# Zeroing the masked triangle on GpSimd after the exponential, in place of a mask matmul before it

## What is computed

```python
def _L1_attn_ref(x, ...):
    ...
    scores = jnp.einsum('bhqd,bhkd->bhqk', q_full, k_full) * scale
    causal = jnp.tril(jnp.ones((T, T), dtype=bool))
    scores = jnp.where(causal[None, None], scores, -jnp.inf)
    probs = jax.nn.softmax(scores, axis=-1)
    y = jnp.einsum('bhqk,bhkd->bhqd', probs, v)
...
x = x + _L1_attn_ref(xn, ...) + _L1_ffn_ref(xn, ...)
```

## Time and profile before

| | us |
|---|---|
| median of 3 runs | 770.57 |
| lowest, highest | 769.31, 770.59 |
| profiled execution | 769.39 |
| its span | 767.6 |
| busy: PE, PEld, DVE, ACT, POOL | 676.4, 541.6, 513.2, 395.2, 355.9 |

### The profile page before, as it was taken

One profiled execution on the slowest core, in us unless ns is written; L12 is line 12 of the kernel. 1 busy time (PEld: TensorE's weight loads), 2 busy tenths in 40 slices (PEclk: granted clock), 3 DMA queues, 4 the chain that ended last, 5 costly groups with the idle time before them and its releaser, 6 DMA issues.

```text
span 767.6 us, 13256 instructions
## 1 busy us (share of the span) xinstructions
PE 676.4 (88%) x4656; PEld 541.6 (71%) x4656; DVE 513.2 (67%) x964; ACT 395.2 (51%) x695; POOL 355.9 (46%) x299
## 2 busy tenths in 40 slices
PE   5898789896976799989989999989989998999996
PEld 4676666886865677767677777667767777777774
DVE  6875746874776656686584867485749577467745
ACT  3644414453552654482765374575446286448263
POOL 1426088386585424153445445164516353315353
PEclk9999899998998999999999999999999999999999
DMA  8336816676976285420005202003303000202100
GB/s 318 115 112 218 266 75 213 211 229 221 340 247 202 77 298 130 158 63 22 2 2 145 49 18 66 2 1 100 94 2 76 9 1 29 73 12 50 34 2 28
DMA packets 66804, 82.76 MB, mean 108 GB/s; under 512 B 7090, under 2 KB 50354, under 8 KB 66738
## 3 DMA queue, kind: packets, MB, share of 16 engines
q1 hardware_dynamic: 63156, 73.39, 30.2%
q0 software_dynamic: 3072, 8.39, 3.3%
q10 hardware_dynamic: 512, 0.13, 0.1%
HBM read 40.34 MB, written 28.84 MB: 90 GB/s over the span
## 4 chain that ended last, share of the span: by engine, by line
PE 43%; ACT 11%; DVE 10%; issue 7%; DMA 2%; POOL 1%; ACTq 1%; SPq 0%; POOLq 0%; DVEq 0%
PE acc L643 4%; PE acc L645 3%; PE acc L644 3%; PE pv L643 3%; PE pm L643 3%; PE ring L965 2%; PE pm L645 2%; PE pm L644 2%; PE pv L645 2%; PE pv L644 2%; DVE hf L2115 2%; PE ring L995 2%; DMA ws<-qs 2%; PE ring L967 2%; ACT act L1448 1%
## 5 line engine op out<-in xcount | busy, mean ns | idle before, releaser
L1558 POOL TENSOR_TENSOR hl<-hf,hh 128x512 fp32r<-128x512 f32 (+1 forms) x76 | 99.2, 1307 | 227.3 <-ACT hh L1247 227.2
L1247 ACT ACTIVATE hh<-hf 128x512 fp32r<-128x512 f32 (+1 forms) x76 | 47.7, 629 | 81.7 <-DVE hf L2115 66.5
L643 PE MATMUL acc<-hh,wh 128*128 128x512 f32 (+1 forms) x168 | 71.1, 423 | 7.6 <-POOL hl L1558 7.6
L2179 DVE TENSOR_REDUCE mx<-ring 128x2 f32<-128x512 f32 (+1 forms) x96 | 61.5, 682 | 9.2 <-PE ring L967 9.2
L645 PE MATMUL acc<-hl,wh 128*128 128x512 f32 (+1 forms) x168 | 66.7, 397 | 0.0
L644 PE MATMUL acc<-hh,wl 128*128 128x512 f32 (+1 forms) x168 | 66.7, 397 | 0.0
L2115 DVE TENSOR_TENSOR hf<-hf,pv 128x512 f32<-128x512 f32 x64 | 43.6, 681 | 34.0 <-PE pv L645 32.6
L1699 POOL TENSOR_TENSOR pl<-act,ph 128x512 f16<-128x512 f32 x32 | 41.6, 1301 | 39.7 <-ACT ph L1453 36.8
L1430 ACT ACTIVATE hf<-pm 128x512 f32<-128x512 f32 x56 | 33.3, 595 | 51.5 <-PE pm L645 51.3
L643 PE MATMUL pv<-xh,wh 128*128 128x512 f32 x128 | 53.7, 419 | 1.8 <-DVE hf L2115 1.5
L645 PE MATMUL pv<-xl,wh 128*128 128x512 f32 x128 | 50.5, 395 | 0.0
(11 more groups left out here) (288 smaller groups left out, 2124.3 us busy)
## 6 DMA issues: line engine op xcount, KB each, us to landing
w4s<-w4hl SPq DMA_DIRECT2D x16, 512.0 KB, 4.5
ws<-qs SPq DMA_DIRECT2D x12, 512.0 KB, 6.0
qT<-qp SPq DMA_DIRECT2D x96, 64.0 KB
kT<-kp SPq DMA_DIRECT2D x96, 64.0 KB
xs<-yg SPq DMA_DIRECT2D x2, 2944.0 KB, 12.4
late<-xs SPq DMA_DIRECT2D x22, 256.0 KB, 3.4
ys<-act SPq DMA_DIRECT2D x22, 256.0 KB, 4.1
stage<-w SPq DMA_DIRECT2D x8, 608.0 KB, 4.6
```

The lines of the kernel that those rows point to most:

```text
L643: pe.matmul(o, w_hi, x_hi, start=first, stop=False, skip_group_check=True)
L1247: a.activation(h_parts(n)[0][0:rows, :], hf[0:rows, n % 2, :], ACT.Copy).then_inc(s_hh, 1)
L1558: return pool.tensor_tensor(dst, src, hi.bitcast(F32), ALU.subtract)
L2179: v.tensor_reduce(mx[:, i, h0:h0 + nh], ring[j % 2][:, :].rearrange("p (n k) -> p n k", n=nh), AX.X, ALU.max).then_inc(s_mx, 1)
```

## The change

The mask matmul and its constant go. Behind each exponential POOL issues one `affine_select`, in place in the fp32 buffer: over the diagonal squares of the fill (two of 128 x 128, or four), it keeps an element where query index - key index >= 0 and writes 0 elsewhere. Both halves of the split now wait for this select (semaphore `triangles_cleared`). On ACT the high half of fill f-1 comes behind the exponential of fill f; on POOL the low half of fill f-2 comes behind the select of fill f. `probs_hi` on DVE waits for the select too. The loads of the small constants are one fewer.

```diff
@@ PE, probs @@
-                        pe.matmul(o, kT[0:SLOT + 2, h, kt * P:(kt + 1) * P], qT[0:SLOT + 2, h, kt * P:SEQ], start=True,
-                                  stop=False, skip_group_check=True)
-                        mm = pe.matmul(o[:, 0:P], ident[:, :], maskk[:, :], start=False, stop=True,
-                                       skip_group_check=True)
+                        mm = pe.matmul(o, kT[0:SLOT + 2, h, kt * P:(kt + 1) * P], qT[0:SLOT + 2, h, kt * P:SEQ],
+                                       start=True, stop=True, skip_group_check=True)
@@ ACT @@
                 a.activation(exps(n), ring[f % 2][:, :], ACT.Exp, scale=SCALE).then_inc(s_e, 1)
-                if n % 3 != 1:
-                    a.wait_ge(s_e, n + 1)
-                    if n >= NP:
-                        a.wait_ge(s_y, (n - NP) // 3 + 1)
-                    a.activation(ph[:, n % NP, :], exps(n), ACT.Copy).then_inc(s_pha, 1)
+
+            def probs_hi(nb, f):
+                n = 12 * nb + f
+                a.wait_ge(s_sel, n + 1)
+                if n >= NP:
+                    a.wait_ge(s_y, (n - NP) // 3 + 1)
+                a.activation(ph[:, n % NP, :], exps(n), ACT.Copy).then_inc(s_pha, 1)
...
                     for f in fills:
                         exponentials(nb, f)
+                        if f and (f - 1) % 3 != 1:
+                            probs_hi(nb, f - 1)
+                        if f == 11:
+                            probs_hi(nb, 11)
@@ POOL @@
+                def clear_triangles(nb, f):
+                    n, heads = 12 * nb + f, 4 if f % 3 == 2 else 2
+                    pool.wait_ge(s_e, n + 1)
+                    square = exps(n).rearrange("p (h q) -> p h q", h=heads)[:, :, 0:P]
+                    pool.affine_select(square, square, [[0, heads], [1, P]], ALU.is_ge, 0.0, base=0,
+                                       channel_multiplier=-1).then_inc(s_sel, 1)
+
+                def probs_part(nb, *fills):
+                    for f in fills:
+                        clear_triangles(nb, f)
+                        if f >= 2 and (f - 2) % 3 != 2:
+                            probs_lo(nb, f - 2)
...
-                probs_lo(b0, 0, 1)
+                probs_part(b0, 0, 1, 2, 3)
                 split_h(n0 + 7, P)
-                probs_lo(b0, 3, 4, 6, 7, 9, 10)
+                probs_part(b0, *range(4, 12))
+                probs_lo(b0, 10)
@@ DVE, probs_hi @@
-                v.wait_ge(s_e, n + 1)
+                v.wait_ge(s_sel, n + 1)
```

More of the change, by code:

```diff
@@ L198, in transformer_blocks @@
         maskq = sb("maskq", [P, P], BF16, c1)
-        maskk = sb("maskk", [P, P], BF16, c1)
         ys = sb("ys", [P, 8, DH + 1], F32, c1)
@@ L290, in transformer_blocks @@
         s_md, s_vsp = sem("max_placed"), sem("values_split")
-        s_sT, s_e, s_y, s_yst, s_yn = map(
-            sem, ("score_bank_turned", "exponentials", "y_bank", "y_steps", "y_normed"))
+        s_sT, s_e, s_sel, s_y, s_yst, s_yn = map(
+            sem, ("score_bank_turned", "exponentials", "triangles_cleared", "y_bank", "y_steps", "y_normed"))
         s_ytr, s_yh, s_yl, s_ao = map(sem, ("y_turned", "y_hi", "y_split", "y_used"))
@@ L518, in small_in @@
                           (gb[:, :], cols), (bout[:, :], bo), (spreadf[:, :], spread_c),
-                          (ident[:, :], identb_c.bitcast(BF16)), (maskq[:, :], mask_c[0].bitcast(BF16)),
-                          (maskk[:, :], mask_c[1].bitcast(BF16)))[i]
+                          (ident[:, :], identb_c.bitcast(BF16)), (maskq[:, :], mask_c.bitcast(BF16)))[i]
                 sp.dma_start(t, src).then_inc(s_const if i else s_bc, 16)
@@ L579, in _ @@
                     x_in(5)
-                if 6 <= q < 14:
+                if 6 <= q < 13:
                     small_in(q - 6)
@@ L952, in scores @@
                         if nb == 0:
-                            pe.wait_ge(s_const, 16 * 9)
+                            pe.wait_ge(s_const, 16 * 8)
                             pe.wait_ge(s_prep, SETUP0 + SETUP1)
@@ L1391, in affine_latents @@
                 if nb == 0:
-                    a.wait_ge(s_const, 16 * 9)
+                    a.wait_ge(s_const, 16 * 8)
                 a.wait_ge(s_ctr, nb + 1)
@@ L1723, in _ @@
                     split_h(n0 + t, P)
-                probs_lo(b1, 0, 1)
+                probs_part(b1, 0, 1, 2, 3)
                 split_h(n0 + 13, P)
-                probs_lo(b1, 3, 4, 6, 7, 9, 10)
+                probs_part(b1, *range(4, 12))
+                probs_lo(b1, 10)
                 split_h(n0 + 14, P)
@@ L2136, in turn_bias @@
             def turn_bias():
-                v.wait_ge(s_const, 16 * 9)
+                v.wait_ge(s_const, 16 * 8)
                 v.tensor_tensor(bqc[:, :, :], gb[:, C_BQ:C_BQ + 4].rearrange("p (i m) -> p i m", i=2),
@@ L2419, in _layouts @@
     bf16 = lambda c: (c.view(np.uint32) >> 16).astype(np.uint16)
-    masks = np.zeros((2, P, P), f)
-    masks[0][np.triu_indices(P, 1)] = MASKED
-    masks[1][np.tril_indices(P, -1)] = MASKED
+    mask = np.zeros((P, P), f)
+    mask[np.triu_indices(P, 1)] = MASKED
     route_c = np.zeros((P, R_COLS), f)
@@ L2433, in _layouts @@
         "ones_c": np.full((P, P), 1.0 / D, f), "ident_c": np.eye(P, dtype=f),
-        "identb_c": bf16(np.eye(P, dtype=f)), "mask_c": bf16(masks), "route_c": route_c,
+        "identb_c": bf16(np.eye(P, dtype=f)), "mask_c": bf16(mask), "route_c": route_c,
         "ones_rows": bf16(np.ones((2, H * SEQ), f)).reshape(2, H, SEQ),
```

## The result

| | median us | runs | range | profiled run / span |
|---|---|---|---|---|
| before | 770.58 | 4 | 769.31 to 771.45 | 769.39 / 767.6 |
| after | 810.19 | 4 | 808.75 to 812.01 | 809.88 / 808.1 |

The changed kernel is slower, 1.0517 times the time before (95% interval 1.049 to 1.0543), by 39.6 us. The forecast was 813 us. Profiled run against profiled run it is +40.5 us, where the walk gave +41.7. The same kernel was run again on another chip beside the experiments: 807.38 us, 1.0484 (1.0466 to 1.0501).

The account below looks back on a forecast made before the run. PE, 88% busy, bounds the kernel, but POOL would bound the probability stage: opening +3.26, two groups +3.73, closing -1.78, sum +5.21 us, times eight +41.7, forecast 813 us. Range for 8 in 10: 788 to 860 us.

Parts of the forecast that it names:

- the walk: Term-by-term timing of one probability stage, from first exponential to ninth up-projection: +5.21 us a stage, times eight +41.7 us.
- opening, to the low half of fill 3: Stage start, first exponential to group 1's first low half: delayed by selects 0 to 5, +3.26 us.
- fills 3 to 9: Two groups in mid-stage, low half of fill 3 to that of fill 9: POOL becomes the bound, +3.73 us.
- closing, to the ninth up-projection: Stage end, from low half 9 to PE's ninth up-projection: 3.48 us instead of 5.26, so -1.78 us.
- The price of a select: On POOL, midway between cast and subtraction: 0.90 us for 512 elements, 0.50 us for 256.
- the cast's end of the walk: Same stage with selects at a one-input cast's price, 0.642 and 0.37 us: +3.47 us a stage, +28 us.
- The group's period: POOL per group of three fills: two low halves, two small selects, a large one and 0.60 for DVE, 4.82 us.
- DVE's turns: Time POOL stands still for DVE's instructions in each group: 0.60 us, 0.30 for each turn.
- The rival with whole turns: DVE's cast, subtraction and product hold POOL for 1.38 us a group instead of 0.60: +19 us, 831 us; 12%.
- The clock: PE's granted clock in the stage: left at 1.00, as the walk's waits are 2.1 us at most.
- dear selects: Each select on POOL costs two passes of the subtraction: +123 us, some 893 us; 13%.
- a faster kernel: Selects fit in POOL's gaps in the stage and PE regains its masks: up to 14.8 us less, 756 us; 3%.

Follow-up runs that it names:

- twice: The changed kernel with every select issued two times, the second behind the first by a semaphore: 854.79 us, 1.1098 against before.
- dve_narrow: The changed kernel with DVE's cast and subtraction for one fill in three covering 32 columns instead of 512: 790.13 us, 1.0253 against before.
- masks_kept: The changed kernel with its selects, waits and new order, but with the 256 mask matmuls put back: 804.64 us, 1.0453 against before.
- neither: The kernel before without mask matmuls and without selects, the exponential's scale a hundredth: 765.90 us, 0.9950 against before.
- filler: The changed kernel with 58 idle 128-column matmuls per probability stage, placed where PE waits: 803.61 us, 1.0436 against before.

## Why the prediction was right, and which steps of it failed

The walk through one stage, term by term (third stage, 462.80 us is 0):

| term | before | predicted | measured |
|---|---|---|---|
| opening, to the low half of fill 3 | 5.91 | 9.17 | 8.14 |
| fills 3 to 9 | 5.91 | 9.64 | 9.08 |
| closing, to the ninth up-projection | 5.26 | 3.48 | 4.12 |
| sum | 17.08 | 22.29 | 21.34 |

- **That POOL becomes the bound, so that the saving is lost: right, and shown.** twice puts nearly the selects' full duration into the time a second time, dve_narrow shortens POOL's instructions and takes 17 to 20 us off, and masks_kept has the same stage. In neither, the removal by itself gave 4 us of its 14.8.
- **The price of a select: mis-sized for the large one.** 0.63 us measured, 0.90 taken, which is just outside the 0.65 to 1.16 that was named as the bound of being right; it is at the cast's end of the walk, where the forecast's own sum was +28 us, about 799. The small ones took 0.41 to 0.46 undisturbed, 0.50 taken. Through 0.20, 0.41 and 0.63 us for 8 (or 4), 256 and 512 elements a line of about 0.20 us and 0.85 ns an element fits. The lower price is most of why the opening came out 1.0 us too long, and it took about 0.4 us off each group (1.9 us of selects taken, 1.5 measured). The Trainium skill (GPSIMD Engine Reference, section 7 on performance pitfalls) gives 2.03 cycles an element for a compare-and-select body and 1.03 when it is unrolled twice. At the 1.2 GHz that the page gives for the engine, the 0.85 ns above are an estimated 1.02 cycles: this case agrees with the unrolled figure.
- **The group's period: right to 4 and 8%.** 4.82 predicted, 4.62 and 4.46 measured. In place of dearer selects it holds a gap of 0.35 us that the walk didn't have: with shorter selects POOL catches up and waits for the exponential of the large fill. The criterion "POOL's work plus 0.6" held but for this gap.
- **DVE's turns: right.** 0.60 a group taken, 0.53 measured by taking them away. The rival with whole turns (1.38 a group, 831 us) is rejected. The Trainium skill (SBUF — State Buffer, "Who interferes with whom") calls the shared port pair an exclusive lock, and says of DVE's two-port modes that the other engine is blocked for the whole instruction. Here POOL lost 0.45 us (0.86 against 0.41) to a two-input subtraction that takes 0.68 alone. That doesn't contradict the page: if the select's 0.20 us of start ran while POOL was blocked, the block would be 0.65 us, an estimate from the line above that no run tests.
- **The closing: 0.64 too short.** The last low half takes 1.60 us with a DVE turn in it (the walk let the values follow the gelu chain), and the 24 value matmuls run at the lower clock: 1.02 us from 483.12 to 484.14, 0.6 before. In masks_kept, whose clock is 1.00 up to there, the ninth up-projection comes 0.5 us sooner, so most of the 0.64 goes with the clock.
- **The clock: failed.** The walk left it at 1.00 because the only fall seen before came with a wait of 5.4 us in one piece, and no wait would be above 2.1. In the changed kernel it fell to 0.50 in or at the end of every stage, and the longest wait was 2.8 us. What PE did ahead of it was wait again and again, work 13.61 us of 19.20. With more for PE to do (masks_kept, filler) the clock holds 1.00 in the stage shown and the time is 3 to 6 us less. One long wait was the wrong thing to look for; how much waiting it takes isn't shown (in dve_narrow PE works 12.73 of 17.72 us of the same stage, and the clock there is 1.00).

So of the three signs that the forecast named as showing it wrong, the large select and the clock came, and the period missed its rule by the gap.

The failures have opposite signs: the walk is 0.95 us a stage too long (7.6 us in eight), and misses what the lower clock costs in the closing and behind the stages. Measured, 8 x 4.26 is 34 of the 40.5 us, and the rest, some 6, lies behind the ninth up-projection. That is where PE runs on at 0.42 us a step instead of 0.23; in masks_kept, where it hardly does, the eight stages' growth (34.4 us) nearly makes up the whole growth of the span (35.9). Without this offset the forecast would have been about 805. The agreement of 813 with 810 is thus in part luck, and better than the walk deserved.

Of the rivals, dear selects, whole DVE turns and a faster kernel are excluded by the durations and by the sign. No kernel measured here with selects beats the one before.

## What to carry to other kernels

Before work is moved from the busiest engine to the idlest, list what both do in the very stage where it lands. PE was 88% busy and POOL 46% over the span; in the stage POOL had 2.2 us of gaps and got 6 us of work, in the middle of a chain. What the removal is worth can be measured alone by leaving the work out (here 4 us, not the 14.8 of the count), and the step on the other engine costs even when it has almost no elements (16 us here, by hop and starts together). And when PE starts to wait often, look at the granted clock in and behind the stretch too.

## What the runs showed of the hardware that was not expected

- A kernel with 256 more matmuls was faster: masks_kept at 804.64 us against 807.38 and 810.19, and filler, with 464 useless ones, at 803.61, all with the same stage to 0.02 us.
- The granted clock went from 1.00 to 0.50 for 3 to 10 us at a time in or at the end of all eight stages, in which no single wait of PE was above 2.8 us.
- A select on POOL over 128x4 f32 takes 0.24 us, over 128x256 0.41 and over 128x512 0.63; two DVE instructions in a group of 4.5 us, of 0.41 and 0.68 us when undisturbed, cost POOL 0.53 us of it.
